# Row maxima and exponentials taken by pairs over two PSUM banks, a second bank for the rotated projections, the opening of expert pages on GpSimd, and side steps at other places of the turn

## The chip, the cores and the metric

The kernel runs on one core of one Trainium2 chip. The metric is the device time of one execution in microseconds, the median of several runs. The core has five engines with queues of their own: PE (TensorE, matmuls), DVE (VectorE), ACT (ScalarE), POOL (GpSimd) and SP (SyncE, which here only issues DMAs). They meet by semaphores.

## What is computed

One transformer block over 16 sequences of 512 positions, 128 channels wide: a layernorm modulated by a condition vector, causal attention of 16 heads with 8 channels each, a gated residual, a second modulated layernorm, and a mixture of 160 experts of which each position takes 8, with a shared expert beside them.

```python
h = _layernorm(x, axis=-1) * (1 + ca) + sa
x = x + ga * attn(h)        # rope on q and k, causal softmax(q k / sqrt(8)) v, projection
h = _layernorm(x, axis=-1) * (1 + cb) + sb
x = x + gb * ffn(h)         # sigmoid router, top 8 of 160, silu experts of width 64, a shared expert
```

## The kernel before

The program is written out in full for each engine: there are no loops at run time. It has two phases. The first is attention with routing, in turns (`turn_a`, i from -2 to 16), one sequence further in each. The second runs the experts over pages of 128 rows, from about 1200 us on; the change leaves it alone.

**One turn.** `core(i)` is the backbone: 20 steps, each with a pair of *max units* of sequence i+1 and a pair of *exp units* of sequences i-1 and i. A unit is one PSUM bank of 512 scores, in causal pieces of heads of one parity (even heads stand on 64 partitions, odd ones on the other 64, so the two units of a pair hold the two halves of PE). Each quarter of a sequence (a quad, 4 heads, `c`) has ten units (`UNITS`), five pairs. In a max unit PE makes the scores (L569) and hides the upper triangle by small matmuls (L577, L582); then DVE takes the row maximum of each block of 128 (`reduce`, L598). The maxima go back into the operands as further rows (`max_end`, L609 to L643), so that in an exp unit PE's products (L680, hidden by L692) come out with the maximum subtracted, and ACT takes the exponential into `prob` (`expo`, L707). `attend` then multiplies by v (L743, bank 5), and ACT and DVE normalise (L752, L764, L769), one quad later, in between the pairs.

**Banks.** Of the eight PSUM banks two belong to the max units (`MX`, unit g in bank g % 2), three to the exp units (`ST`, unit g in bank 2 + g % 3), one to `attend` (`PV`), and one each to the steps before attention (`MA`) and after it (`MB`). PE's `begin` holds a unit back until the unit that had its bank is done with:

```python
wait(e, s_mxd, n * 4 * UNITS + g - 1)           # max unit g: unit g-2 is reduced
wait(e, s_exa, n * 4 * UNITS + g - prev + 1)    # exp unit g: unit g-3 has its exponential
```

`pair(u0, u1)` orders PE's work as: wait and first product of u0, wait and first product of u1, then the remaining products and hiding matmuls in turn.

**Side steps.** All else of the turn is cut into steps that `merge` places between the backbone's by a number from 0 to 1: `pre(i+2)` (layernorm, the projections q, q rotated, k, k rotated and v, all through bank `MA`: L452, L463, L518, with DVE's rope L458, L467 between them; and the split into bf16 parts with POOL's L486, L495), the loads and stores of SP (`exp_loads` L661, `max_loads` L551, stores L507, `clears` L382), the routing of sequences i-1 and i-2 (`to_logits`, `post`), and POOL's scatters of rows into pages (L818), paced by the backbone's semaphores. `PRE_AT`, `FIRST_AT`, `SECOND_AT` and their `_LATE` are the tables of places. An engine takes its steps strictly in this order.

**Paging.** In `post`, eleven DVE operations on one partition of 160 values (`paging`, L1036 to L1051) turn the counts of rows for each expert into page places. The last four (`fill`, `curd1`, `curd2`, `open`) prepare what the next sequence starts from. `keep` then writes the row positions twice, as `pos_s` (L1142, for the scatters) and `pos_all` (L1143, for the expert phase).

## Time and profile before

| | |
|---|---|
| median of 3 runs | 2020.71 us (2019.48 to 2025.43) |
| the profiled execution | 2040.86 us, of which the span of the trace is 2038.9 us |
| PE, DVE, ACT, POOL busy in the span | 77%, 58%, 41%, 50% |
| mean granted TensorE clock | 0.887 |
| first and last L609 (end of a sequence's maxima) | 87.7 and 1099.5 us, 16 of them |

The first 1100 us or so are the turns and the rest, from about 1200 us, the experts. The interval from one L609 to the next is the length of a turn. Busy shares alone say little here, since each engine waits for the others within a step; the questions are what each pair of units waits for, and how long the things take that the change joins or moves.

### The profile page before, as it was taken

What the parts mean: (1) busy time and instruction counts of PE and PEld (TensorE: products, weight loads), DVE (VectorE), ACT (ScalarE), POOL (GpSimd) and SP (SyncE); (2) the same over time, 40 slices, a digit from 0 to 9 for tenths busy, and PEclk for the clock granted to TensorE, in tenths of its full rate; (3) what the DMA queues carried; (4) which work ended last, traced back from release to release, by engine and by line L of the source; (5) the groups of instructions that cost most, each with busy time, mean ns of one, the idle gap of its engine ahead of it and who ended that gap; (6) DMA issues with size and microseconds to landing.
All of it is one profiled execution on the core that took longest, in us unless ns stands there. A gap on an engine that the chain in (4) does not pass through costs nothing.

```text
span 2038.9 us, 35388 instructions
## 1 busy us (share of the span) xinstructions
PE 1565.4 (77%) x12102; PEld 792.8 (39%) x12102; DVE 1185.1 (58%) x2998; ACT 826.2 (41%) x1717; POOL 1021.8 (50%) x1057
## 2 busy tenths in 40 slices
PE   5558877788788778877877668966888888888875
PEld 2224433343343334333333345643444444444431
DVE  4657876687678767777766526633444444444434
ACT  1045544453445445445544434323343333343421
POOL 2001355555665556555645510056666666666663
PEclk9989888997898779778977678978999999999988
DMA  5695455554555545545542258986777777777631
GB/s 161 178 303 159 140 150 149 167 158 141 158 167 157 143 135 168 143 140 170 168 113 74 79 188 283 334 274 185 240 237 229 212 240 222 239 239 239 207 106 56
DMA packets 264986, 369.70 MB, mean 181 GB/s; under 512 B 41207, under 2 KB 141832, under 8 KB 264680
## 3 DMA queue, kind: packets, MB, share of 16 engines
q1 hardware_dynamic: 214248, 268.81, 45.5%
q0 software_dynamic: 28672, 58.78, 9.5%
q10 hardware_dynamic: 21888, 39.86, 5.2%
q8 instruction: 98, 1.61, 0.3%
q14 instruction: 80, 0.66, 0.1%
HBM read 219.69 MB, written 147.60 MB: 180 GB/s over the span
## 4 chain that ended last, share of the span: by engine, by line
PE 46%; DVE 20%; issue 12%; another core or an unknown queue 12%; ACT 5%; SPq 2%; DMA 2%; ACTq 1%; POOL 1%; DVEq 0%
DVE block_max L598 9%; PE bank L1715 6%; PE bank L743 5%; PE bank L1739 4%; PE bank L1578 4%; PE bank L1557 3%; PE bank L1594 3%; PE bank L569 3%; PE bank L680 2%; ACT prob L707 2%; PE bank L692 2%; PE bank L452 2%; PE bank L582 2%; PE bank L1720 1%
## 5 line engine op out<-in xcount | busy, mean ns | idle before, releaser
L1646 POOL DMA_INDIRECT vh<-results,pos_all x448 | 454.3, 1014 | 351.6 <-PE bank L1313 125.3
L818 POOL DMA_INDIRECT pages<-h,pos_s x448 | 433.2, 967 | 262.5 <-issue 103.7
L598 DVE TENSOR_REDUCE block_max<-bank 128x4 f32<-128x512 f32 x640 | 411.9, 683 | 245.7 <-PE bank L582 112.6
L707 ACT ACTIVATE prob<-bank 128x512 f32<-128x512 f32 x640 | 349.4, 598 | 465.9 <-PE bank L692 245.3
L1733 DVE TENSOR_TENSOR work<-work,bank 128x512 f32<-128x512 f32 x160 | 110.1, 688 | 358.1 <-issue 187.8
L569 PE MATMUL bank<-km,qm 64*128 64x512 bf16 (+3 forms) x1024 | 203.2, 343 | 112.2 <-DVE block_max L598 65.7
L680 PE MATMUL bank<-qe,ke 64*128 64x512 bf16 (+3 forms) x1024 | 174.9, 341 | 96.3 <-issue 57.2
L743 PE MATMUL bank<-prob,v_ext 128*32 128x512 f32 (+3 forms) x2048 | 225.7, 506 | 8.3 <-issue 5.3
L1608 ACT ACTIVATE v_ext<-bank 128x256 f32<-128x256 f32 x254 | 87.0, 387 | 199.9 <-remote 84.3
L569 PEld LDWEIGHTS bank<-km,qm 64*128 64x128 bf16 x1024 | 51.6, 97 | 276.6 <-issue 164.6
L1594 PE MATMUL bank<-prob,ke 64*128 64x128 f32 x1216 | 114.4, 309 | 52.3 <-ACT ke L1586 37.0
L1727 ACT ACTIVATE work<-bank 128x512 f32<-128x512 f32 x160 | 96.2, 601 | 143.2 <-PE bank L1715 77.2
L1594 PEld LDWEIGHTS bank<-prob,ke 64*128 64x128 f32 x1216 | 84.8, 197 | 141.5 <-issue 84.1
L680 PEld LDWEIGHTS bank<-qe,ke 64*128 64x128 bf16 x1024 | 50.1, 99 | 224.0 <-issue 153.9
L1715 PE MATMUL bank<-vh,on_att 128*128 128x512 f32 x160 | 88.4, 636 | 35.4 <-issue 28.5
L1578 PE MATMUL bank<-qe,prob 128*64 128x128 f32 x1216 | 105.3, 297 | 12.5 <-issue 9.2
L692 PE MATMUL bank<-cb_all 64*128 64x128 bf16 (+1 forms) x1280 | 112.6, 226 | 0.0
L1557 PE MATMUL bank<-c_all,prob 128*128 128x128 f32 x608 | 104.8, 297 | 2.9 <-issue 1.5
L1586 ACT ACTIVATE ke<-bank 128x256 f32<-128x256 f32 x152 | 58.6, 385 | 117.7 <-remote 71.0
L413 POOL TENSOR_TENSOR rstd<-var,mhalf 128x4 f32<-128x4 f32 x16 | 16.5, 1032 | 162.8 <-DVE var L407 162.8
L486 POOL TENSOR_TENSOR work<-work,shelf 128x512 f32<-128x512 f32 x32 | 36.9, 1153 | 121.6 <-ACT shelf L480 121.6
L692 PEld LDWEIGHTS bank<-cb_all 64*128 64x128 bf16 x1280 | 75.3, 106 | 31.1 <-issue 11.7
(221 smaller groups left out, 2542.4 us busy)
## 6 DMA issues: line engine op xcount, KB each, us to landing
prob<-wexp SPq DMA_DIRECT2D x448, 96.0 KB
pages<-free_rows SPq DMA_DIRECT2D x38, 1024.0 KB
prob<-pages SPq DMA_DIRECT2D x152, 256.0 KB
results<-v_ext ACTq DMA_DIRECT2D x152, 256.0 KB
qm<-q_stacks SPq DMA_DIRECT2D x64, 256.0 KB
km<-k_stacks SPq DMA_DIRECT2D x64, 256.0 KB
qe<-q_stacks SPq DMA_DIRECT2D x64, 256.0 KB
ke<-k_stacks SPq DMA_DIRECT2D x64, 256.0 KB
```

The lines of the kernel that those rows point to most:

```text
L569: e.matmul(MX[g % 2][:, c0:c0 + (i + 1) * P], qm[rows_, c % 2, h, i * P:(i + 1) * P], km[rows_, c % 2, h, 0:(i + 1) * P], start=(k == 0), ...
L598: e.tensor_reduce(block_max[:, at, :], MX[g % 2][:, :].rearrange("p (k t) -> p k t", t=P), AX.X, ALU.max).then_inc(s_mxd, 1)
L680: e.matmul(ST[g % 3][:, c0:c0 + S - j * P], ke[rows_, c % 2, h, j * P:(j + 1) * P], qe[rows_, c % 2, h, j * P:S], start=(k == 0), stop=Tru ...
L692: return e.matmul(out_, pick[rows_, :], over, start=False, stop=True, skip_group_check=True)
L707: e.activation(prob[:, slot, :], ST[g % 3][:, :], ACT.Exp, scale=SCALE).then_inc(s_exa, 1)
L743: last = e.matmul(PV[32 * g:32 * g + 32, j * P:S], v_ext[:, j, 4 * c + g, :], prob[:, (c % 2) * UNITS + u, c0:c0 + S - j * P], start=(j == ...
L818: e.indirect_dma_start(out=pages, in_=h2[:, t, :], in_offset=None, out_offset=bass.IndirectOffsetOnAxis(ap=pos_s[:, t * TOPK + k:t * TOPK ...
L1557: last = e.transpose(TX[G % 2][:, :].rearrange("d (p q) -> d q p", q=GRP)[:, q, :], x_in[G % DEEP][:, q, :], ident)
L1578: last = e.matmul(GT[half:half + 64, (j // 2) * P:(j // 2 + 1) * P], w_gate(G, j), x_T[G % 2][:, j * P:(j + 1) * P], start=True, stop=True)
L1594: last = e.matmul(YP[j % 2][:, (j // 2) * D:(j // 2 + 1) * D], h_g[G % 2][half:half + 64, (j // 2) * P:(j // 2 + 1) * P], w_down(G, j), st ...
L1646: e.indirect_dma_start(out=y8[:, i, k, :], out_offset=None, in_=results[0:ready(n) * GRP * P, :], in_offset=bass.IndirectOffsetOnAxis(ap=p ...
L1715: e.matmul(FG[:, :], fw[v % 4][:, c0:c0 + P], vh[:, PAGED + m, :], start=True, stop=True).then_inc(s_dg, 1)
```

## The change

1. The two max units of a pair, now always in `max_banks[:, 0]` and `[:, 1]`, raise one semaphore, and DVE reduces both with one instruction. PE starts a pair when the whole pair before it is reduced. Likewise the exp units: two banks instead of three, one exponential of 1024 columns for a pair, and PE starts a pair when the exponential of the whole pair before it is done. The semaphores count pairs.
2. The bank that this frees (`MC`, bank 4) takes the rotated projections. So the second projection of q no longer waits for DVE to have read the first, and k's first waits for q's first only.
3. `fill`, `curd1`, `curd2` and `open` leave DVE; six operations on POOL (`open_pages`) take their place.
4. `pos_s` is gone; the scatters read `pos_all`.
5. The tables of places are other ones, also for SP's loads; `SECOND_AT` has 13 entries, not 14, and the pacing of scatters ends at 0.306 of a turn, not 0.4.

```diff
-        block_max = sb("block_max", [P, 40, NT])
+        block_max = sb("block_max", [P, 2, 20, NT])
...
-        pos_s = sb("pos_s", [P, NT * TOPK], U32)
...
+        opened = sb("opened", [1, NE])
-        bank = [ctx.enter_context(nc.psum_tensor(f"bank{i}", [P, 512], F32)) for i in range(8)]
-        MX, ST, PV, MA, MB = bank[0:2], bank[2:5], bank[5], bank[6], bank[7]
+        max_banks = ctx.enter_context(nc.psum_tensor("max_banks", [P, 2, S], F32))
+        exp_banks = ctx.enter_context(nc.psum_tensor("exp_banks", [P, 2, S], F32))
+        bank = [b[:, i, :] for b in (max_banks, exp_banks) for i in range(2)] + \
+            [ctx.enter_context(nc.psum_tensor(f"bank{i}", [P, 512], F32)) for i in range(4, 8)]
+        MX, ST, MC, PV, MA, MB = bank[0:2], bank[2:4], bank[4], bank[5], bank[6], bank[7]
...
                 def proj_a(e, w=w, prev=prev):
...
-                        pre_d.wait(e, prev + "_b", n)
+                        pre_d.wait(e, prev + "_a", n)
                     pre_p.done(e.matmul(MA[:, :], col["w" + w], hT[:, :], start=True, stop=True), w + "_a")
...
                 def proj_b(e, w=w):
-                    pre_d.wait(e, w + "_a", n)
-                    pre_p.done(e.matmul(MA[:, :], col["w" + w + "r"], hT[:, :], start=True, stop=True), w + "_b")
+                    if w == "k":
+                        pre_d.wait(e, "q_b", n)
+                    else:
+                        pre_d.wait(e, "k_b", n - 1)
+                    pre_p.done(e.matmul(MC[:, :], col["w" + w + "r"], hT[:, :], start=True, stop=True), w + "_b")
...
             def v_proj(e):
-                pre_d.wait(e, "k_b", n)
+                pre_d.wait(e, "k_a", n)
...
         def max_unit(n, g):
...
-                wait(e, s_mxd, n * 4 * UNITS + g - 1)
+                wait(e, s_mxd, n * 2 * UNITS + g // 2)
...
-                    hide(e, 1).then_inc(s_mxp, 1)
+                    last = hide(e, 1)
+                    if u % 2 == 1:
+                        last.then_inc(s_mxp, 1)
             def reduce(e):
-                e.wait_ge(s_mxp, n * 4 * UNITS + g + 1)
-                if g == 0:
+                if u % 2 == 0:
+                    return
+                e.wait_ge(s_mxp, n * 2 * UNITS + g // 2 + 1)
+                if g == 1:
                     fin_d.wait(e, "i0", n - 1)
-                at = (u % 4 // 2 * 16 + par * 8 + 2 * c + u // 4) if u < 8 else 32 + 4 * par + c
-                e.tensor_reduce(block_max[:, at, :], MX[g % 2][:, :].rearrange("p (k t) -> p k t", t=P),
+                at = (u % 4 // 2 * 8 + 2 * c + u // 4) if u < 8 else 16 + c
+                e.tensor_reduce(block_max[:, :, at, :], max_banks[:, :, :].rearrange("p b (k t) -> p b k t", t=P),
                                 AX.X, ALU.max).then_inc(s_mxd, 1)
...
         def exp_unit(n, g):
...
-            prev = 3 if g >= 3 else g + 4 * UNITS - max(k for k in range(4 * UNITS) if k % 3 == g % 3)
...
-                wait(e, s_exa, n * 4 * UNITS + g - prev + 1)
+                wait(e, s_exa, n * 2 * UNITS + g // 2)
...
             def expo(e):
-                e.wait_ge(s_exp, n * 4 * UNITS + g + 1)
-                if u == 0:
+                if par == 0:
+                    return
+                e.wait_ge(s_exp, n * 2 * UNITS + g // 2 + 1)
+                if u == 1:
                     wait(e, s_pv, 4 * n + c - 1)
-                slot = (c % 2) * UNITS + exp_place(pieces[0][0], par, pieces[0][1])[0]
-                e.activation(prob[:, slot, :], ST[g % 3][:, :], ACT.Exp, scale=SCALE).then_inc(s_exa, 1)
+                slot = (c % 2) * UNITS + exp_place(pieces[0][0], 0, pieces[0][1])[0]
+                e.activation(prob[:, slot:slot + 2, :], exp_banks[:, :, :], ACT.Exp, scale=SCALE).then_inc(s_exa, 1)
...
-                ("filled", lambda e: e.tensor_scalar(filled[:, :], fill[:, :], -float(P), None, ALU.add)),
-                ("fill", lambda e: e.scalar_tensor_tensor(out=fill[:, :], in0=newp[:, :], scalar=-float(P),
-                                                          in1=total[:, :], op0=ALU.mult, op1=ALU.add)),
-                ("curd1", lambda e: e.scalar_tensor_tensor(out=curd[:, :], in0=endp[:, now, :], scalar=float(P),
-                                                           in1=rows[:, now, 1, :], op0=ALU.mult, op1=ALU.subtract)),
-                ("curd2", lambda e: e.scalar_tensor_tensor(out=curd[:, :], in0=newp[:, :], scalar=0.0, in1=curd[:, :],
-                                                           op0=ALU.is_gt, op1=ALU.mult)),
-                ("open", lambda e: e.tensor_tensor(rows[:, then, 1, :], rows[:, now, 1, :], curd[:, :], ALU.add)))
+                ("filled", lambda e: e.tensor_scalar(filled[:, :], fill[:, :], -float(P), None, ALU.add)))
+
+            any_row = eb_row[:, :]
+            opening = (
+                ("taken", lambda e: e.tensor_scalar(opened[:, :], newp[:, :], float(P), None, ALU.mult)),
+                ("any", lambda e: e.tensor_scalar(any_row, newp[:, :], 1.0, None, ALU.min)),
+                ("fill", lambda e: e.tensor_tensor(fill[:, :], total[:, :], opened[:, :], ALU.subtract)),
+                ("past", lambda e: e.tensor_tensor(opened[:, :], rows[:, now, 0, :], opened[:, :], ALU.add)),
+                ("last", lambda e: e.tensor_tensor(opened[:, :], opened[:, :], any_row, ALU.mult)),
+                ("open", lambda e: e.tensor_tensor(rows[:, then, 1, :], rows[:, now, 1, :], opened[:, :], ALU.add)))
...
                 if k == 0:
                     P_.wait(e, "cnt", n)
+                    G_.wait(e, "open", n - 1)
...
+            def open_pages(e):
+                D_.wait(e, "filled", n)
+                for k, (name, f) in enumerate(opening):
+                    if k > 1:
+                        G_.wait(e, opening[k - 1][0], n)
+                    G_.done(f(e), name)
...
-            steps.append({"pe": spread, "act": spread_keep, "sp": lambda e: ends_store(e, n)})
+            steps.append({"pe": spread, "act": spread_keep, "pool": open_pages, "sp": lambda e: ends_store(e, n)})
...
             def keep(e):
                 D_.wait(e, "pos1", n)
-                wait(e, s_scat, 16 * NT * TOPK * n)
-                D_.done(e.tensor_scalar(pos_s[:, :], pos8[:, :, :].rearrange("p t k -> p (t k)"), -TAKEN, None, ALU.add), "pos_s")
...
-        PRE_AT = (0.021, 0.061, 0.15, 0.207, 0.274, 0.36, 0.422, 0.474, 0.481, 0.553, 0.611, 0.636, 0.688, 0.751)
+        PRE_AT = (0.030, 0.085, 0.163, 0.227, 0.303, 0.351, 0.425, 0.475, 0.477, 0.558, 0.616, 0.654, 0.692, 0.752)
...
-                streams.append((exp_loads(i, (0,)), 0.03, 0.03))
-                streams.append((exp_loads(i, (1,)), 0.28, 0.28))
-                streams.append((exp_loads(i, (2,)), 0.53, 0.53))
-                streams.append((exp_loads(i, (3,)), 0.78, 0.78))
+                streams.append((exp_loads(i, (0,)), 0.101, 0.101))
+                streams.append((exp_loads(i, (1,)), 0.223, 0.223))
+                streams.append((exp_loads(i, (2,)), 0.546, 0.546))
+                streams.append((exp_loads(i, (3,)), 0.640, 0.640))
```

The table `PRE_AT` stands for the others (`PRE_LATE`, `FIRST_AT`, `FIRST_LATE`, `SECOND_AT`, `SECOND_LATE`), most of whose entries move by less than 0.03 of a turn.

On **PE**, in the middle of a steady turn, between the products with v of one quad (L743; L754 in the new numbering), stand a max pair and an exp pair. `bank0` and `bank1` are `MX`, `bank2` to `bank4` are `ST`. Before:

```order
L743 MATMUL bank5<-prob,v_ext 32x128 [waits s_exa]
L743 MATMUL bank5<-prob,v_ext 32x128 x3
L569 MATMUL bank0<-km,qm 128x512 [waits s_mxd]
L569 MATMUL bank1<-km,qm 128x512 [waits s_mxd]
L577 MATMUL bank0<-cb_all 128x64
...
L743 MATMUL bank5<-prob,v_ext 32x256 x3
L680 MATMUL bank2<-qe,ke 128x512 [waits s_exa]
L680 MATMUL bank3<-qe,ke 128x512 [waits s_exa]
L692 MATMUL bank2<-cb_all 128x64
```

and now, at the same place:

```order
L754 MATMUL bank5<-prob,v_ext 32x128 [waits s_exa]
L754 MATMUL bank5<-prob,v_ext 32x128 x3
L574 MATMUL max_banks<-km,qm 128x512 [waits s_mxd] x2
L582 MATMUL max_banks<-cb_all 128x64 x4
L754 MATMUL bank5<-prob,v_ext 32x256 [waits s_exa]
L754 MATMUL bank5<-prob,v_ext 32x256 x3
L687 MATMUL exp_banks<-qe,ke 128x512 [waits s_exa] x2
L699 MATMUL exp_banks<-cb_all 128x64 x4
```

PE's matmuls and their order are the same; what the waits of L574 and L687 ask for is now a whole pair, and the exp pair uses the same two banks each time.

On **DVE**, at the paging of a steady turn (names: `fill`, `total`, `newp` and `endp` are rows of 160 counts). Before:

```order
L1039 SCALAR_TENSOR_TENSOR endp<-newp,endp,zero_row 1x160 [waits post_d,s_ends]
L1041 TENSOR_TENSOR curd<-endp,newp 1x160 [waits post_d]
L1042 SCALAR_TENSOR_TENSOR rows_deep<-curd,rows_deep 1x160 [waits post_d]
L598 TENSOR_REDUCE block_max<-bank 128x4 [waits s_mxp] x2
L421 TENSOR_SCALAR work<-xr,mv,rstd 128x128 x2
L1044 TENSOR_SCALAR filled_deep<-fill 1x160 [waits post_p]
L1045 SCALAR_TENSOR_TENSOR fill<-newp,total 1x160 [waits post_d]
L1047 SCALAR_TENSOR_TENSOR curd<-endp,rows_deep 1x160 [waits post_d]
L1049 SCALAR_TENSOR_TENSOR curd<-newp,curd 1x160 [waits post_d]
L1051 TENSOR_TENSOR rows_deep<-rows_deep,curd 1x160 [waits post_d]
L598 TENSOR_REDUCE block_max<-bank 128x4 [waits s_mxp] x2
```

and now on DVE:

```order
L1050 SCALAR_TENSOR_TENSOR endp<-newp,endp,zero_row 1x160 [waits s_ends,post_d]
L1052 TENSOR_TENSOR curd<-endp,newp 1x160 [waits post_d]
L1053 SCALAR_TENSOR_TENSOR rows_deep<-curd,rows_deep 1x160 [waits post_d]
L607 TENSOR_REDUCE block_max<-max_banks 128x2x4 [waits s_mxp]
L1055 TENSOR_SCALAR filled_deep<-fill 1x160 [waits post_p]
L423 TENSOR_SCALAR work<-xr,mv,rstd 128x128 x2
L607 TENSOR_REDUCE block_max<-max_banks 128x2x4 [waits s_mxp]
```

with these on POOL, between two scatters (L829) of sequence i-2's rows:

```order
L1059 TENSOR_SCALAR opened<-newp 1x160 [waits post_d]
L1060 TENSOR_SCALAR eb_row<-newp 1x160
L1061 TENSOR_TENSOR fill<-total,opened 1x160 [waits post_g]
L1062 TENSOR_TENSOR opened<-rows_deep,opened 1x160 [waits post_g]
L1063 TENSOR_TENSOR opened<-opened,eb_row 1x160 [waits post_g]
L1064 TENSOR_TENSOR rows_deep<-rows_deep,opened 1x160 [waits post_g]
L829 DMA pages<-h,pos_all 77824x128 [waits s_mxp]
```

Four operations went from ahead of a reduction on DVE, and six came in ahead of a scatter on POOL.

## Rows read from the trace of the kernel before

**Rows 1.** The page: busy time of each engine in the span
```profile
PE 1565.4 (77%) x12102; PEld 792.8 (39%) x12102; DVE 1185.1 (58%) x2998; ACT 826.2 (41%) x1717; POOL 1021.8 (50%) x1057
```
**Rows 2.** Windows, one turn: length; PE, PEld, DVE, ACT, POOL busy; clock
```profile
476.10:545.60 69.50, 55.24 (x506) 26.59 (x505) 50.62 (x148) 31.76 (x63) 39.60 (x43) 0.84 0.53 154
```
**Rows 3.** The chain that ended last, 290 to 965 us, shares by line
```profile
by line: DVE block_max L598 17.2%; issue 11.4%; PE bank L743 8.5%; another core or an unknown queue 5.0%; PE bank L569 4.8%; PE bank L680 4.7%; PE bank L692 3.2%; PE bank L452 3.1%; PE bank L582 2.9%; ACT prob L707 2.4%; PE bank L950 1.9%; 
```
**Rows 4.** Waits, 290 to 965 us: who for whom, us, times, longest
```profile
PEld bank L569 <- DVE block_max L598: 36.5, 81, 1.5
...
PEld bank L680 <- ACT prob L707: 30.9, 35, 6.4
...
PE bank L569 <- DVE block_max L598: 28.0, 56, 1.5
...
PE bank L680 <- ACT prob L707: 14.3, 4, 6.2
```
**Rows 5.** Groups of instructions by shape: busy us, mean ns
```profile
L598 DVE TENSOR_REDUCE block_max<-bank 128x4 f32<-128x512 f32 x640 | 411.9, 683 | 245.7 <-PE bank L582 112.6 <-remote 89.8 <-PE bank L577 39.9
L707 ACT ACTIVATE prob<-bank 128x512 f32<-128x512 f32 x640 | 349.4, 598 | 465.9 <-PE bank L692 245.3 <-remote 211.6 <-issue 7.0
...
L1656 DVE TENSOR_TENSOR vh<-vh,wts_all 128x1024 f32<-128x1024 f32 x56 | 68.4, 1221 | 0.1
...
L1568 ACT ACTIVATE qe<-bank 128x512 f32<-128x512 f32 x102 | 61.3, 601 | 40.1 <-remote 29.9 <-PE bank L1557 9.2 <-issue 1.0
L1586 ACT ACTIVATE ke<-bank 128x256 f32<-128x256 f32 x152 | 58.6, 385 | 117.7 <-remote 71.0 <-PE bank L1578 38.6 <-issue 8.0
...
L1664 DVE TENSOR_TENSOR vh<-vh 128x512 f32<-128x512 f32 x56 | 38.5, 687 | 0.3
```
**Rows 6.** Timeline, one step of a turn: start us, us
```profile
502.46 1.28 DVE L598 TENSOR_REDUCE block_max<-bank 128x4 f32<-128x512 f32 x2
502.99 1.08 ACT L707 ACTIVATE prob<-bank 128x512 f32<-128x512 f32 x2 [2.11 <-PE bank L692]
...
503.20 0.39 PE L569 MATMUL bank<-km,qm 64*128 64x512 bf16 x1 [0.43 <-DVE block_max L598]
...
503.80 0.39 PE L569 MATMUL bank<-km,qm 64*128 64x512 bf16 x1 [0.21 <-DVE block_max L598]
```
**Rows 7.** Timeline, DVE's four last paging operations
```profile
627.75 0.31 DVE L1045 SCALAR_TENSOR_TENSOR fill<-newp,total 1x160 f32<-1x160 f32 x1
...
628.80 0.31 DVE L1051 TENSOR_TENSOR rows_deep<-rows_deep,curd 1x160 f32<-1x160 f32 x1
```
**Rows 8.** Timeline: pos_s and pos_all on DVE, the smallest operations on POOL
```profile
509.24 0.17 DVE L1142 TENSOR_SCALAR pos_s<-pos 128x32 uint32<-128x32 f32 x1
509.32 0.18 DVE L1143 TENSOR_SCALAR pos_all<-pos 128x32 uint32<-128x32 f32 x1
...
510.82 0.45 POOL L1158 TENSOR_TENSOR hit<-hit 128x128 f32<-128x128 f32 x1
...
511.73 0.25 POOL L1162 TENSOR_TENSOR wts_all<-hit 128x32 f32<-128x32 f32 x1
```
**Rows 9.** The line L463 (rotated projections): what PE waited for, whole span
```profile
  DVE work L458: 10.3, 8
```
**Rows 10.** Timeline, the stall near a turn's end
```profile
601.95 0.39 PE L680 MATMUL bank<-qe,ke 64*128 64x512 bf16 x1 [0.87 <-issue]
...
604.84 1.09 ACT L707 ACTIVATE prob<-bank 128x512 f32<-128x512 f32 x2 [6.06 <-remote]
605.01 1.29 DVE L598 TENSOR_REDUCE block_max<-bank 128x4 f32<-128x512 f32 x2 [5.19 <-remote]
...
605.49 0.61 PE L680 MATMUL bank<-qe,ke 64*128 64x512 bf16 x1 [3.16 <-issue]
```
**Rows 11.** Windows ahead of and behind that stall
```profile
605.50:621.50 16.00, 12.64 (x84) 5.35 (x84) 13.14 (x55) 6.06 (x13) 6.59 (x8) 0.50 0.38 97
587.60:601.60 14.00, 11.96 (x131) 6.67 (x131) 9.55 (x29) 8.94 (x18) 11.21 (x12) 1.00 0.56 182
```

More of the change, by code:

```diff
@@ L814, in scatter @@
             if t == 0 and k == 0:
-                post_d.wait(e, "pos_s", n)
+                post_d.wait(e, "pos_all", n)
                 post_a.wait(e, "h2", n)
@@ L1062, in page_op @@
                     wait(e, s_ends, 16 * n)
-                    D_.wait(e, "curd1", n - 1)
                 if name == "filled":
```

83 lines of the change are left out of this document (40 added, 43 removed).

## The prediction, made before the changed kernel was timed

> **What bounds the kernel now.** I read the page first: no engine is full, PE is busy for 77% of the span and DVE for 58% [rows 1]. That is a mean over two phases, and the change touches the turns alone. So next the windows of one turn: of 69.5 us PE is busy for 55.2, DVE for 50.6, ACT for 31.8, POOL for 39.6, at a granted clock of 0.84 [rows 2]. PE and DVE are both near what the turn takes, ACT and POOL are not. The chain over some ten turns says which of them the end hangs on: 17.2% of it is DVE's reductions, the largest share of any line, while the exponentials have 2.4%; 11.4% is "issue", time in which PE waits for nothing that is shown [rows 3]. The waits agree: PE's loads for the max units waited 81 times for DVE and its matmuls 56 times, for the exp units 35 and 4 times for ACT [rows 4]. The timeline of one step shows how this goes: DVE takes two reductions in 1.28 us from 502.46, PE's first product starts at 503.20, behind the first of them, its second only at 503.80, behind the other [rows 6]. A step is thus a loop from PE to DVE and back, with side work of both between.
>
> **Joining the reductions.** A pair costs 1.28 us [rows 6]. One of 1024 columns isn't in the trace. DVE's other operation of that length takes 1221 ns against 687 for 512 columns, so 534 ns for 512 more; with 683 for the reduction of one bank that is 1217 ns [rows 5]. 320 pairs by 0.06 us are 20 us of DVE's time. The bound on the one side is nothing (no gain from joining), on the other the whole fixed part of an operation, 687 - 534 = 153 ns a pair, 49 us. PE loses nothing of its own by waiting for the whole pair: its first product now starts later, but the second, which ended last anyway, starts up to 0.06 us earlier.
>
> **Joining the exponentials.** Two cost 1.08 us [rows 6]; one of 1024 columns, by ACT's 601 ns for 512 and 385 for 256, is 598 + 2 * 216 = 1030 ns [rows 5]: 0.05 us by 320, 16 us of ACT. With ACT's exponentials at 2.4% of the chain, about 16 of 675 us, where they are busy for some 390 * 0.598 = 233 (40 a turn, and 675 / 69 = 9.8 turns), a fifteenth of that counts: 1 us. The Trainium skill ("ScalarE: Activation LUTs", section "What ACT_TABLE_LOAD costs") gives 186 ns fixed, 0.833 ns a column and an overlap of 93 ns between neighbours. By that the saving would be 93 ns a pair, 30 us of ACT and 2 us of the sum; our rows of 1.08 us show less to be saved, and I stay with them.
>
> **Paging and pos_s.** DVE's four last paging operations run from 627.75 to 629.11, 1.36 us [rows 7], in 14 sequences: 19 us. `pos_s` delays what follows by 0.08 us [rows 8], 1 us in all. So DVE is relieved of 20 + 19 + 1 = 40 us. What share of it counts? In the 675 us of the chain's window L598 has 116 us [rows 3]; its instructions there are about 40 in 69 us by 683 ns, 267 us busy. So 43% of DVE's time lies on the chain, and of 40 us I take 17.
>
> **POOL.** Six operations on one partition of 160 values, each behind a wait for the one before. The nearest rows are 0.25 us for 32 columns and 0.45 for 128, on 128 partitions [rows 8]: 1.5 to 3 us a turn. They stand ahead of a scatter, and behind the wait for `filled`. POOL idles for 30 us of a turn [rows 2], which hides them, and their results are needed a turn later: 0. If that cover were gone (a scatter that ACT's `back_keep` awaits becomes late), it is at most 14 * 3 = 42 us.
>
> **The bank MC.** The rotated projections no longer wait for DVE's rope of the plain ones. PE waited 10.3 us for that in the whole span [rows 9]. The bounds are 0 and 10.3; I take half, 5 us, since DVE's own work stays.
>
> **The third exp bank.** This is the price. Before, the second product of a pair waited for the first exponential of the pair before, now for both: 1030 - 598 = 0.43 us later, wherever PE was held by ACT. Rows name 39 such waits in 675 us [rows 4]; over the sixteen sequences' turns that makes some 64, by 0.43 us 27 us. Behind an exp pair PE meets a max pair, and there it often waits for DVE (81 to 137 waits on some 195 pairs [rows 4]), which absorbs the delay. I take 60% as absorbed: +11 us. The bounds are 0 and all 320 pairs, 137 us.
>
> **The places.** PE's order of matmuls is nearly the same, the side steps move by a row or a few. SP's load of the fourth quad now stands at 0.640 and waits there for its buffer, free at about 0.735; behind it on SP stand a clear and k's store, which have until the next turn. I cost that at 0: the first loads needed have a quarter turn. What the moves are worth elsewhere has no row. Their nearest measure is the stall that recurs near a turn's end, 3.16 us on PE [rows 10]: gone in fifteen turns it would be 47 us, doubled as much the other way. I take 0 and keep both.
>
> **The sum.** -17 - 1 - 5 + 11 = -12 us on the profiled execution's 2040.86, so 2029. That execution stands 20 us above the median of the runs shown, 2020.7; the same 12 us off the median give **2008**.
>
> **The rivals.**
>
> *The exp pair becomes the loop (slower).* With one set of banks, PE's exp pair, ACT's exponential and PE's next exp pair can't overlap at all. Every lateness of ACT (its side steps, 0.6 us and more each, stand in one queue with the exponentials) is passed on to PE undamped. For it: the four waits of PE for ACT took 14.3 us, up to 6.2 each [rows 4], and some of the "issue" ahead of L680 may be ACT's. Against it: ACT is busy for under half the turn. My gains are 23 us, so it decides once 54 pairs of 320 pass on 0.43 us. If a third do, 107 pairs, it is 46 - 23 = +23 us: 2044.
>
> *DVE's relief becomes idleness (no change).* If the step's length is PE's own work and its unexplained waits, what DVE saves is waited away, and -5 meets +11 with a remnant of the 17: 2015 to 2027, say 2021. The chain's 11.4% of "issue" speaks for it, the 17.2% of reductions against.
>
> *The stall and the clock (much faster).* In the stall DVE and ACT both sit idle for over 5 us until about 605, and PE resumes at 605.49 [rows 10]. Before it the clock was 1.00 (2.4 GHz), in the 16 us behind it 0.50 (1.2 GHz) [rows 11], and the same 512-column product takes 0.61 us instead of 0.39 [rows 10]. At a mean of 0.84, a third of the turn runs at half clock [rows 2]. In 16 us there PE is busy for 12.6; at full clock this would be 12.6 * 0.39 / 0.61 = 8.1, 4.5 us less [rows 11]. If other places break the stall in most turns, and half of that reaches the end, it is 2.3 + 0.5 * 3.16, some 3.9 us in ten turns: 2008 - 39, about 1970. Against it: nothing in the change names the stall's cause. The Trainium skill ("TensorE: Matmul & The Clock Gate", section "HAM oscillation — how this bites in real kernels") says that pauses of PE put it to half rate, paid again at each. By this rule the trace agrees here, with half clock right behind the stall; the same rule makes it dearer if single exp banks add pauses.
>
> *The change doesn't do what it says:* the PSUM operand over two banks could be taken more slowly than its columns. At 1.28 us for the joined reduction and 1.08 for the exponential nothing is won there, and the sum is -12 + 9 + 1 = -2, in with "no change".
>
> **The numbers.** Within 0.3%, 6 us, is what a measurement of this kernel can't tell from no change. Chances: forecast 0.41, stall and clock 0.12, no change 0.17 (with the change that doesn't do what it says), the exp pair 0.30. Faster is thus 0.53, the same 0.17, slower 0.30. The range reaches to about 1965, the stall's rival, and to 2045, the exp rival at a third of the pairs; beyond stand more pairs than that, or a POOL without cover, 2 in 10 or less. The likeliest case's own range is 1990 to 2014: DVE's full 40 us on the chain and none of it.
>
> **What would show it.** Right: the joined reduction near 1.22 us and the exponential near 1.03, DVE's busy time 35 to 45 us lower, the line of reductions still the largest on the chain, L468's wait for DVE gone, waits of the exp products for ACT up to 60 or 80 per ten turns and no more than 0.5 us each on the whole. Wrong: turns (from one end of maxima to the next) that are longer than 69 us with PE waiting for ACT in most exp pairs; or a row of scatters or `rstd` late on POOL behind the opening; or a mean clock in the turns away from 0.85 by more than 0.03, which would say that pauses of PE, and not the joined operations, made the difference.

## The result, and the profile after

| | before | changed |
|---|---|---|
| median | 2022.12 us (2019.48 to 2025.43, 4 runs) | 2061.60 us (2060.28 to 2063.01, 4 runs) |
| ratio | | 1.0195 (95%: 1.0172 to 1.0219), slower; whether by 2% is within the noise |
| span of the profiled execution | 2038.9 us | 2061.2 us |

The profiled execution of before stands 19 us above its median, that of the changed kernel 1 us above. So the two traces differ by 22 us only; the other 17 us of the 39.5 between the medians can't be placed in them.

The page of the changed kernel, against [rows 1]:

```profile
PE 1513.2 (73%) x12102; PEld 774.4 (38%) x12102; DVE 1156.2 (56%) x2608; ACT 809.0 (39%) x1397; POOL 1076.8 (52%) x1141
```

DVE has 29 us less to do, ACT 17, and POOL 55 more. The joined operations cost what rows of before had said (1217 and 1030 ns), namely 1220 and 1024 ns (by shape; busy us, mean ns | idle before, and what ended it), against [rows 5]:

```profile
L607 DVE TENSOR_REDUCE block_max<-max_banks 128x8 f32<-128x1024 f32 x320 | 390.5, 1220 | 295.7 <-remote 153.8 <-PE max_banks L587 99.9 <-PE max_banks L582 33.2
L718 ACT ACTIVATE prob<-exp_banks 128x1024 f32<-128x1024 f32 x320 | 327.6, 1024 | 459.3 <-PE exp_banks L699 268.3 <-remote 178.7 <-issue 9.7
```

So less work, and yet more time. The windows say where: one steady turn, against [rows 2].

```profile
479.30:552.10 72.80, 50.05 (x505) 24.91 (x505) 49.08 (x124) 31.93 (x46) 44.54 (x50) 0.85 0.56 149
```

72.8 us for 69.5, at the same clock (0.85, 0.84). Counted by the ends of the maxima (L617, before L609), the changed kernel is ahead by 3 us at the first, 4.6 at the second and 5.1 at the third (199.87 against 204.99), in turns that have no scatters yet; it then loses some 3 us in most turns and stands 28 us behind at the last (1127.70 against 1099.55). The experts behind it take no longer (933.5 against 939.4 us).

The waits of PE, 290 to 965 us, against [rows 4] (us in total, times, longest):

```profile
PE max_banks L574 <- DVE block_max L607: 79.8, 76, 2.7
PE exp_banks L687 <- issue: 45.8, 25, 5.1
PE exp_banks L687 <- ACT prob L718: 34.6, 23, 7.2
PE bank L1035 <- DVE chosen L999: 14.7, 8, 1.8
```

PE's matmuls wait for DVE three times as long as before (28.0), for ACT more than twice (14.3), and newly for the choice of experts (L999) ahead of the count. But DVE is not busier. What DVE waits for says more. DVE's waits, 337 to 1055 us, first of before, then of the changed kernel:

```profile
DVE block_max L598 <- PE bank L582: 63.7, 36, 3.8
DVE block_max L598 <- remote: 63.3, 23, 5.4
```

```profile
DVE block_max L607 <- remote: 125.6, 37, 8.0
DVE block_max L607 <- PE max_banks L587: 50.5, 31, 4.7
```

"Remote" is an idle time at whose end no instruction of this core ended: by the profile, the operand had been there for long. It doubled. The same word stood in [rows 5] already, 89.8 us ahead of the reductions and 211.6 ahead of the exponentials, and I had read past it. What it is, the timeline of the changed kernel shows near a turn's end (the place of [rows 10]):

```profile
607.72 0.28 PE L699 MATMUL exp_banks<-cb_all 64*128 64x128 bf16 x4
...
608.51 0.22 PE L582 MATMUL max_banks<-cb_all 64*128 64x64 bf16 x4
...
612.61 0.96 POOL L829 DMA_INDIRECT pages<-h,pos_all  x1 [0.30 <-issue]
613.72 1.02 ACT L718 ACTIVATE prob<-exp_banks 128x1024 f32<-128x1024 f32 x1 [6.06 <-remote]
...
614.80 0.61 PE L687 MATMUL exp_banks<-qe,ke 64*128 64x512 bf16 x2 [5.06 <-issue]
...
616.62 1.23 DVE L607 TENSOR_REDUCE block_max<-max_banks 128x8 f32<-128x1024 f32 x1 [7.92 <-remote]
```

The exp pair is ready at 608.00; its exponential starts at 613.72. The max pair is ready at 608.73; its reduction starts at 616.62. ACT and DVE are idle all the while, and so, from 609.7, is PE. I call this a **late signal**.

The trace holds more than its views show: the time of each semaphore's update. In the kernel before, 912 of the 2385 updates that PE gave came over 0.3 us behind the last end of a matmul that gives that semaphore, none of them ahead of the first scatter. Of the 2941 updates by ACT, DVE and POOL not one did. So it is what comes from PE that is late, and the reader starts at once when it comes. Whether PE's signal is late or the matmul's result itself can't be told, since the profile models the ends of matmuls; "ready" above is by such an end.

The Trainium skill ("Perfetto Trace Analysis", section "Per-instruction lifecycle: what the profiler-reported window actually captures") says that waiting for a semaphore and its propagation lie outside what a profiled instruction shows. By that, such a delay has no row of its own, and the trace agrees: in the views it shows only as idle time with no cause on the core (6.06 and 7.92 us above).

### The profile page after: what moved, and what is told of

Same layout as the page of the kernel before. It is cut to its first block and busy times, and to the rows that moved or that the text cites. A ratio compares the mean times of both kernels' runs of the same rounds, so it can differ in the third digit from the quotient of the medians.

```text
span 2061.2 us, 34762 instructions
## 1 busy us (share of the span) xinstructions
PE 1513.2 (73%) x12102; PEld 774.4 (38%) x12102; DVE 1156.2 (56%) x2608; ACT 809.0 (39%) x1397; POOL 1076.8 (52%) x1141
## 3 DMA queue, kind: packets, MB, share of 16 engines
q0 software_dynamic: 28672, 58.78, 9.4%
## 5 line engine op out<-in xcount | busy, mean ns | idle before, releaser
L829 POOL DMA_INDIRECT pages<-h,pos_all x448 | 438.7, 979 | 225.4 <-issue 123.7
L607 DVE TENSOR_REDUCE block_max<-max_banks 128x8 f32<-128x1024 f32 x320 | 390.5, 1220 | 295.7 <-remote 153.8
L718 ACT ACTIVATE prob<-exp_banks 128x1024 f32<-128x1024 f32 x320 | 327.6, 1024 | 459.3 <-PE exp_banks L699 268.3
L574 PE MATMUL max_banks<-km,qm 64*128 64x512 bf16 (+3 forms) x1024 | 145.9, 347 | 182.2 <-DVE block_max L607 149.7
L754 PE MATMUL bank<-prob,v_ext 128*32 128x512 f32 (+3 forms) x2048 | 229.7, 502 | 11.9 <-issue 9.5
L687 PE MATMUL exp_banks<-qe,ke 64*128 64x512 bf16 (+3 forms) x1024 | 144.1, 342 | 126.2 <-issue 61.0
L1609 PE MATMUL exp_banks<-prob,ke 64*128 64x128 f32 x608 | 115.9, 315 | 46.7 <-ACT ke L1601 23.9
L574 PEld LDWEIGHTS max_banks<-km,qm 64*128 64x128 bf16 x1024 | 37.5, 98 | 297.4 <-DVE block_max L607 154.4
L687 PEld LDWEIGHTS exp_banks<-qe,ke 64*128 64x128 bf16 x1024 | 39.5, 100 | 240.9 <-issue 164.7
L1593 PE MATMUL exp_banks<-qe,prob 128*64 128x128 f32 x1216 | 105.0, 296 | 10.6 <-issue 7.3
L1572 PE MATMUL max_banks<-c_all,prob 128*128 128x128 f32 x608 | 104.8, 297 | 1.2 <-issue 0.9
L699 PE MATMUL exp_banks<-cb_all 64*128 64x128 bf16 (+1 forms) x1280 | 91.8, 225 | 0.0
L1754 PE MATMUL bank<-work,on_att 128*128 128x512 f32 x160 | 89.9, 645 | 0.0
```

The lines of the kernel that those rows point to most:

```text
L574: e.matmul(MX[par][:, c0:c0 + (i + 1) * P], qm[rows_, c % 2, h, i * P:(i + 1) * P], km[rows_, c % 2, h, 0:(i + 1) * P], start=(k == 0), st ...
L607: e.tensor_reduce(block_max[:, :, at, :], max_banks[:, :, :].rearrange("p b (k t) -> p b k t", t=P), AX.X, ALU.max).then_inc(s_mxd, 1)
L687: e.matmul(ST[par][:, c0:c0 + S - j * P], ke[rows_, c % 2, h, j * P:(j + 1) * P], qe[rows_, c % 2, h, j * P:S], start=(k == 0), stop=True, ...
L718: e.activation(prob[:, slot:slot + 2, :], exp_banks[:, :, :], ACT.Exp, scale=SCALE).then_inc(s_exa, 1)
L754: last = e.matmul(PV[32 * g:32 * g + 32, j * P:S], v_ext[:, j, 4 * c + g, :], prob[:, (c % 2) * UNITS + u, c0:c0 + S - j * P], start=(j == ...
L829: e.indirect_dma_start(out=pages, in_=h2[:, t, :], in_offset=None, out_offset=bass.IndirectOffsetOnAxis(ap=pos_all[:, n, t * TOPK + k:t * ...
```

## The experiments

They ran in five batches, each on another chip, and the kernel before ran beside them each time. Its median tells the chips apart: 2024 to 2043 us on four, as in the main comparison (2022), and 1784 us on one. No batch was repeated on its chip, so a lasting property of a chip can't be told from its condition at that time. Ratios are to before on the same chip. "Remote" is the sum of the profile's rows on the reductions and on the exponentials (DVE + ACT, us); "none" is said of these two groups.

| run | what it is | ratio (95%) | before there | remote |
|---|---|---|---|---|
| changed kernel | | 1.0195 (1.0172 to 1.0219) | 2022 | 153.8 + 178.7 |
| a_old_places | changed, all old places | 1.0106 (1.0074 to 1.0139) | 2040 | 86.5 + 177.7 |
| c_new_places | before, all new places | 1.0259 (1.0227 to 1.0291) | 2040 | 139.5 + 212.9 |
| d_open_pool | before, opening on POOL | 1.0046 (1.0022 to 1.0069) | 2040 | 91.5 + 210.9 |
| e_max_pairs | before, maxima by pairs | 0.9971 (0.9953 to 0.9989) | 2040 | 81.5 + 201.6 |
| after_again | changed | **0.9920** (0.9898 to 0.9943) | **1784** | none |
| g_pairs_only | changed, old places, opening on DVE | 1.0016 (0.9994 to 1.0037) | 1784 | none |
| f_exp_pairs | before, exponentials by pairs | 1.0116 (1.0081 to 1.0150) | 1784 | none |
| n_choose_back | changed, cut and choice back | 0.9909 (0.9890 to 0.9929) | 1784 | none |
| t_first_back | changed, first half's places back | 1.0080 (1.0051 to 1.0109) | 2042 | 118.3 + 195.9 |
| t_pre_back | changed, `PRE_*` back | 1.0304 (1.0272 to 1.0335) | 2042 | 134.4 + 236.9 |
| t_loads_back | changed, SP's loads back | 1.0215 (1.0179 to 1.0251) | 2042 | 145.4 + 177.7 |
| t_second_back | changed, `SECOND_*` back | 1.0178 (1.0150 to 1.0207) | 2042 | 147.7 + 220.0 |
| x_before_plain | before, plain DMAs for the scatters | 0.9350 (0.9326 to 0.9375) | 2024 | none |
| x_after_plain | changed, plain DMAs for the scatters | 0.9269 (0.9245 to 0.9293) | 2024 | none |
| p_first_new | before, first half's new places | 0.9969 (0.9950 to 0.9988) | 2024 | 98.7 + 174.6 |
| u_two_back | changed, first half's places and opening back | 1.0097 (1.0069 to 1.0125) | 2024 | 102.3 + 147.0 |
| y_max_first | before, maxima by pairs and first half's new places | 0.9967 (0.9945 to 0.9988) | 2043 | 99.4 + 166.7 |
| f_exp_again | before, exponentials by pairs | 1.0072 (1.0050 to 1.0093) | 2043 | 68.8 + 130.7 |

**Parts and places.** Three theories: the single set of exp banks, POOL's opening, or the places. The expectations name times by the main comparison's 2022 us; ratios go over to another chip better.

> The changed kernel with the places of before: the same tables of side steps, loads and pacing (one of the two entries 0.175 for paging dropped, since there are three paging steps now). Theory 'single exp set' (the third exp bank's loss costs the 3 us a turn): stays at 2050 to 2065. Theory 'opening on POOL' (the six operations, 3.5 us a turn on POOL, delay scatters or the row they stand ahead of): also 2050 to 2065. Theory 'places' (the new tables cost it): falls by 25 to 45, to 2020 or 2035, and PE's new waits at the count for `chosen` (some 2 us a turn) are gone. Those waits alone, 14 by 2, would be 28 us.

The edit, and the reverse of it in c_new_places:

```diff
-        FIRST_AT = (0.519, 0.548, 0.562, 0.646, 0.675, 0.678, 0.703, 0.734, 0.766, 0.792, 0.824, 0.850, 0.858, 0.902, 0.902, 0.978, 0.982)
+        FIRST_AT = (0.535, 0.548, 0.573, 0.646, 0.668, 0.721, 0.723, 0.729, 0.776, 0.796, 0.85, 0.851, 0.859, 0.909,
+                    0.91, 0.939, 0.964)
...
```

> The kernel before with the new places alone (the fourth paging step right beside the third). Theory 'places': slower by 20 to 40, 2042 to 2062, PE waits for `chosen` ahead of the count. Theories 'single exp set' and 'opening on POOL': within 8 of before, 2014 to 2030.

> The kernel before with the opening on POOL alone. Theory 'opening on POOL': slower by 20 to 45, 2042 to 2067, all in turns with scatters. Theories 'single exp set' and 'places': DVE's 19 us of relief by its 43% share of the chain, so faster by 0 to 10, 2012 to 2022; POOL's busy time 50 us higher, without effect.

```diff
-            steps.append({"pe": spread, "act": spread_keep, "sp": lambda e: ends_store(e, n)})
+            steps.append({"pe": spread, "act": spread_keep, "pool": open_pages, "sp": lambda e: ends_store(e, n)})
```

> The kernel before with the maxima by pairs alone (and the scatters reading pos_all): three single exp banks, opening on DVE, old places. All three theories: the joined reduction costs 1.22 us for 1.28, so 20 us of DVE by 43%: faster by 5 to 12, 2010 to 2017. If instead the loss lies in the joined maxima (PE's first product of a pair now waits for the whole pair), it is slower, 2030 to 2060, with long waits of L574's successor for DVE.

```diff
-                e.tensor_reduce(block_max[:, at, :], MX[g % 2][:, :].rearrange("p (k t) -> p k t", t=P),
+                e.tensor_reduce(block_max[:, :, at, :], max_banks[:, :, :].rearrange("p b (k t) -> p b k t", t=P),
```

The places are a large part: 0.009 of the changed kernel's 1.0195 (give or take 0.004, and from two chips), and 1.0259 when put on the kernel before. With them goes the remote idle time of DVE, 86.5 us with old places against 153.8 in the changed kernel, and 139.5 with new places against 89.8 in the kernel before. With the old places:

```profile
L607 DVE TENSOR_REDUCE block_max<-max_banks 128x8 f32<-128x1024 f32 x320 | 390.6, 1221 | 280.5 <-PE max_banks L587 121.0 <-remote 86.5 <-PE max_banks L582 54.5
```

and with the new ones on the kernel before:

```profile
L598 DVE TENSOR_REDUCE block_max<-bank 128x4 f32<-128x512 f32 x640 | 412.0, 683 | 272.1 <-remote 139.5 <-PE bank L582 96.8 <-PE bank L577 29.4
```

No theory was borne out in size. With the old places the changed kernel came down by 18 us, where the theory of the places asked for 25 to 45 and the others for none. The kernel before went up by 53 with the new ones, more than the 20 to 40 expected. The opening cost 9, under the 20 to 45 of its own theory. Only the joined maxima came in as expected (0.9971, so 6 us faster).

The opening costs 1.0046, where all theories but its own had 0.995 to 1.0: DVE's busy time fell by 16 us (to 1168.9; 19 was asked), and nothing was paid for it. Its six operations run one after another from 566.78 to 570.68 us, 3.9 us, on POOL, which issues the scatters:

```profile
566.78 0.63 POOL L1059 TENSOR_SCALAR opened<-newp 1x160 f32<-1x160 f32 x1
567.40 0.61 POOL L1060 TENSOR_SCALAR eb_row<-newp 1x160 f32<-1x160 f32 x1
568.09 0.51 POOL L1061 TENSOR_TENSOR fill<-total,opened 1x160 f32<-1x160 f32 x1
...
569.87 0.81 POOL L1064 TENSOR_TENSOR rows_deep<-rows_deep,opened 1x160 f32<-1x160 f32 x1
```

The two left out are of the kind of L1061, 0.51 and 0.52 us. I had taken 0.25 to 0.5 us for one. The Trainium skill ("GPSIMD Engine Reference", section "3.1 Elementwise — side-by-side cycle accounting") gives 2.6 cycles an element at 1.2 GHz for two inputs; for 160 elements that is an estimate of 0.35 us before any fixed part. The trace agrees in so far as the two-input operations, 0.51 us at the least, lie above it; what the rest is no run here shows, and the one-input ones took no less (0.61 and 0.63).

**The same kernel on another chip.** The next runs were meant to size what was left.

> The changed kernel again, as the measure for the others on this chip. 1.0195 of before as first measured; between 1.014 and 1.025.

> The changed kernel with the opening on DVE and the places of before: what is left is both joinings, the bank MC and pos_s. With the old places and the opening on POOL the ratio was 1.0106, and the opening alone cost 1.0046. Theory 'single exp set': 1.004 to 1.010, turns of 70 to 71 us, PE waiting some 6 us a turn for ACT. Theory 'the opening is all that is left': 0.995 to 1.002.

> The kernel before with the exponentials by pairs alone (and the scatters reading pos_all), bank 4 unused, single maxima. Theory 'single exp set': slower by 10 to 35, 1.005 to 1.017, with more waits of PE's exp products for ACT. My prediction's terms give -1 + 11 = +10, its rival +23 and more. Theory 'joined units are both harmless alone': 0.997 to 1.003.

```diff
-                e.activation(prob[:, slot, :], ST[g % 3][:, :], ACT.Exp, scale=SCALE).then_inc(s_exa, 1)
+                e.activation(prob[:, slot:slot + 2, :], exp_banks[:, :, :], ACT.Exp, scale=SCALE).then_inc(s_exa, 1)
```

> The changed kernel with its last two routing steps of a turn (the second cut and the choice) back from 0.978 and 0.982 to 0.939 and 0.964, nothing else. Theory 'the late choice is what the new places cost': PE's waits for it at the count (some 2 us a turn, 14 turns) go, ratio lower than the changed kernel's by 0.007 to 0.013. Rival, 'it only stands ahead of another wait' (PE would meet DVE or ACT a few rows on): within 0.003 of the changed kernel.

The first of these expectations was missed altogether, and that opened the case: here the kernel before takes 1784 us and the changed kernel 1771, **13 us less**. The prediction's sum was -12. The same two groups, on this chip:

```profile
L607 DVE TENSOR_REDUCE block_max<-max_banks 128x8 f32<-128x1024 f32 x320 | 390.0, 1219 | 141.2 <-PE max_banks L587 85.4 <-PE max_banks L582 50.3 <-issue 0.5
L718 ACT ACTIVATE prob<-exp_banks 128x1024 f32<-128x1024 f32 x320 | 327.4, 1023 | 262.3 <-PE exp_banks L699 251.2 <-issue 6.2
```

The joined operations take the same time to 1 ns; "remote" is gone, and of 1968 updates that PE gave none was over 0.3 us late. The timeline at the same place of the program as above:

```profile
538.97 0.28 PE L699 MATMUL exp_banks<-cb_all 64*128 64x128 bf16 x4
...
539.29 1.02 ACT L718 ACTIVATE prob<-exp_banks 128x1024 f32<-128x1024 f32 x1 [0.79 <-issue]
...
539.76 0.22 PE L582 MATMUL max_banks<-cb_all 64*128 64x64 bf16 x4
...
540.03 1.23 DVE L607 TENSOR_REDUCE block_max<-max_banks 128x8 f32<-128x1024 f32 x1 [0.48 <-PE max_banks L582]
```

0.04 us from the end of the exp pair to the exponential, where it was 5.72. The turn takes 58.3 us instead of 71.8:

```profile
487.83:546.10 58.27, 46.89 (x505) 23.27 (x505) 48.93 (x124) 31.41 (x46) 44.39 (x50) 0.91 0.66 187
```

With g at 1.0016, the new places and the opening together gain 0.010 here, where they lost. The joined exponentials alone cost 1.0116, as their theory said: a real price, but one that the other parts pay for here. The choice moved back (n) changes nothing here, as its rival said.

**Which table.** Back on a chip with late signals (before 2042 us):

> The changed kernel with the places of the first routing half back. Two chips have shown two pictures: where before takes 2020 to 2040 us (long stops of PE at fixed places of the turn), all new places together cost the changed kernel 0.009 of before; where before takes 1784 us (no such stops) the changed kernel is at 0.992. Theory 'one table carries it, the first half's' (late choice, 2 us a turn of waits): on a chip with stops 1.008 to 1.014 instead of 1.0195. Theory 'the stops carry it, and any table shifts them': 1.013 to 1.022. On a chip without stops both say 0.989 to 0.996.

> The changed kernel with the places of the steps before attention back. Theory 'first half': stays at 1.017 to 1.022 on a chip with stops. Theory 'the stops': the stop of a turn stands after the 17th pair of maxima, where these steps end in the stores of k; 10.1 us from the 17th to the 18th reduction in the changed kernel, 7.3 with all old places. If this table moves it, 1.010 to 1.016 and under 8.5 us there. Without stops 0.989 to 0.998.

> The changed kernel with the five places of SP's loads back. Theory 'first half': 1.017 to 1.022 on a chip with stops. Theory 'the loads': an earlier fourth load blocks SP, so that the store of k is issued later and its burst meets PE's fetch; 1.010 to 1.016. Without stops 0.989 to 0.996.

> The changed kernel with the places of the second routing half back (and its pacing left). Both theories of the first half and of the loads: unchanged, 1.017 to 1.022 on a chip with stops, 0.989 to 0.996 without. If this table carries it, 1.008 to 1.014 with stops.

The first routing half's places carry it: 1.0080, as low as with all old places. Those of `SECOND_*` and of the loads don't, and the new `PRE_*` even help by 0.011. That was in no theory. The pacing of the scatters and the place of the maxima's end were not moved back by themselves. I had blamed the late choice; but with it back, PE still waited for `chosen` for 10.6 us in ten turns, and what fell was DVE's remote time, 153.8 to 118.3. Where in the turn it lies I worked out from the timelines, as the time from one reduction's end to the next, median of eight turns: from the 17th pair to the 18th it is 7.4 us before, 10.1 in the changed kernel, about 7 with all old places and with those of the first half (single turns 3 to 9), and 2.8 on the chip without late signals.

The sum of "remote" is no price list, though. The kernel before with joined exponentials, run again below (f_exp_again), has 199.5 us of it and is slower than before (1.0072), the kernel before with the first half's new places has 273.3 and is faster (0.9969).

**What the signals are late for.** In the program none is late until the first scatter: in before the first scatter is at 237.2 us and the first exponential over 0.3 us late at 241.5, in the changed kernel 231.8 and 236.0. The next two kernels leave out the rows' way to their experts' pages: the same 64 KB go to fixed places, by a plain DMA in place of the indirect one.

> The kernel before with its 448 scatters (rows to computed places, through POOL's indirect DMA) replaced by plain DMAs of the same 64 KB to fixed places of the same pages, issued by POOL at the same points of the order; the rows thus don't go to the pages of their experts. Theory 'late signals come with the scatters': DVE and ACT start up to 8 us after PE's last matmul, in 212 us of before's turns, only after the first scatter of the program; with plain DMAs this falls under 30 us and the turns from 68.5 to under 60 us. Rival 'late signals come with the traffic of DRAM as such': 150 us or more stay. On a chip without late signals: 0.99 to 1.01 of before by POOL's lighter work.

> The changed kernel with the same replacement. Theory 'late signals turn the verdict': over the kernel before with plain DMAs its time is 0.987 to 0.996, as on the chip without late signals (0.992), wherever it runs. Rival 'the places cost by themselves on such chips': 1.01 or more over the kernel before with plain DMAs.

```diff
-            e.indirect_dma_start(
-                out=pages, in_=h2[:, t, :], in_offset=None,
-                out_offset=bass.IndirectOffsetOnAxis(ap=pos_all[:, n, t * TOPK + k:t * TOPK + k + 1], axis=0),
-            ).then_inc(s_scat, 16)
+            first = (n * NT * TOPK + t * TOPK + k) * P
+            e.dma_start(pages[first:first + P, :], h2[:, t, :]).then_inc(s_scat, 16)
```

On a chip with late signals (before 2024 us) they vanish from the turns of both kernels. The groups of before with plain DMAs, and then of the changed kernel with them:

```profile
L598 DVE TENSOR_REDUCE block_max<-bank 128x4 f32<-128x512 f32 x640 | 410.5, 682 | 146.2 <-PE bank L582 108.2 <-PE bank L577 37.8
L707 ACT ACTIVATE prob<-bank 128x512 f32<-128x512 f32 x640 | 347.9, 599 | 274.8 <-PE bank L692 274.2
L819 POOL DMA_DIRECT2D pages<-h x448 | 243.1, 545 | 282.0 <-PE bank L692 119.0 <-PE bank L582 102.0 <-PE bank L577 42.6
```

```profile
L607 DVE TENSOR_REDUCE block_max<-max_banks 128x8 f32<-128x1024 f32 x320 | 390.1, 1219 | 148.0 <-PE max_banks L587 99.2 <-PE max_banks L582 44.5
L718 ACT ACTIVATE prob<-exp_banks 128x1024 f32<-128x1024 f32 x320 | 327.7, 1024 | 286.0 <-PE exp_banks L699 281.1
L830 POOL DMA_DIRECT2D pages<-h x448 | 244.1, 548 | 185.9 <-PE exp_banks L699 72.2 <-PE max_banks L582 52.5 <-PE max_banks L587 40.6
```

The queue, its bytes (58.78 MB, half of them the scatters') and its packets (28672) are the same, so it is not the amount of traffic. Two things went together with the indirect form and aren't told apart: POOL is held for 548 instead of 979 ns by an issue, and the rows go to places side by side instead of scattered ones.

The same executions hold a second test that I hadn't planned. In the expert phase these kernels still gather rows by POOL's indirect DMAs, and there the late signals are back. In the kernel before with plain scatters, not one of 1565 updates by PE from 237 us on was over 0.3 us late until the first gather at 1188.1 us; from there on 373 of 566 were, the first at 1193.8. Two of ACT's groups in that phase:

```profile
L1606 ACT ACTIVATE v_ext<-bank 128x256 f32<-128x256 f32 x254 | 86.8, 384 | 214.7 <-PE bank L1592 90.5 <-remote 72.6 <-issue 51.2
...
L1584 ACT ACTIVATE ke<-bank 128x256 f32<-128x256 f32 x152 | 58.5, 385 | 120.1 <-remote 82.4 <-PE bank L1576 36.8 <-issue 0.9
```

From the first gather to the end it takes 702 us here and 707 in the kernel before as it was, so nearly all of what was won was won ahead of it.

The turns fall to about 60 and 59 us. And the verdict turns: 1879.01 / 1894.85 = **0.992** (about 0.988 to 0.995 by the two intervals), the value of the other chip. Both were foretold by the theory of late signals; the rivals named in the two expectations are out.

**Parts, again.**

> The kernel before with the new places of the first routing half alone. Putting them back in the changed kernel took 1.0195 to 1.008. Theory 'the first half's places cost it where signals are late': 1.008 to 1.02 on such a chip, 0.995 to 1.003 where none are late. Rival 'they cost only together with the single exp banks': 0.997 to 1.004 on either.

> The changed kernel with two parts back: the places of the first routing half, and the opening on DVE. A candidate for both kinds of chip. By 1.008 less 0.0046 for the opening: 1.001 to 1.006 where signals are late; 0.988 to 0.998 where none are.

> The exponentials by pairs alone, again, on this chip: 1.0116 where no signal was late. Theory 'late signals make the single set dear': 1.015 to 1.03 where they are late. Rival 'the set costs the same everywhere': 1.008 to 1.015. By differences of the runs on chips with late signals (1.0106 less 0.0046 for the opening, plus 0.003 for the maxima) it would be 1.009.

> The kernel before with the two parts that were each 0.997 of it where signals are late: maxima by pairs (0.9971) and the new places of the first routing half (0.9969). If the two add up: 0.992 to 0.996. If both take away the same wait (DVE ahead of the reductions at the turn's end): 0.996 to 0.999. Without late signals 0.985 to 0.998.

The rival held in the first: these places gain 0.003 on the kernel before and cost only in company. u_two_back was missed. With the first half's places back, the opening's return to DVE won nothing that shows (1.0097 against 1.0080), so the 1.0046 is no fixed price that could be subtracted. The joined exponentials alone cost 1.0072, not more than the 1.0116 without late signals; that theory falls. Whether the two single gains add up stays open: 0.9967 (0.9945 to 0.9988) was measured, 0.994 would be their sum, with as wide an interval. Where signals are late, this kernel is ahead of before and of the changed one, though of before by little more than such a comparison resolves; where none are late it was not run, and the changed kernel beats before by 0.008.

## Why the prediction was wrong

It forecast 2008 us, faster; the time is 2061.6, above the range's 2045. What it said about the length of the joined instructions held. Its sum, -12, was met on the chip that delivers signals at once (-13), but in part by luck: there the joined exponentials cost +21 instead of +10, and the places, costed at nothing, gained with the opening some 17. By its own steps, in us, on chips with late signals (ratio times 2040, each give or take 4 to 8; from two chips besides that of the main comparison):

| step | forecast | measured |
|---|---|---|
| joined reductions, pos_s | -9 | -6 (e alone, 0.9971) |
| opening: DVE's relief -8, POOL 0 | -8 | +9 (d alone, 1.0046) |
| joined exponentials with one set of banks | -1 + 11 | +15 (f alone, 1.0072) |
| bank MC and what the parts do together | -5 | +4 (what is left of a, 1.0106, by subtraction) |
| places | 0 | +18 (1.0195 less 1.0106) |
| sum | -12 | +39.5 |

- **The places: the first step that failed.** I took "0 and keep both", with the stall as the measure, at 3.16 us on PE and in sum 47 us a kernel; they cost 18. The stall was the right object, and its size was wrong: before has 301 us of remote idle time on the two groups of instructions alone, at several places of a turn, and with the moved side steps DVE's share of it went from 86.5 to 153.8 us. In the range I let the exp rival at 2045 stand for the slower side, and the stall's own bound of +47 (2055) didn't enter it. Even that would have been too low, since two more steps had the wrong sign.
- **The single exp set: right in sign, price half as large again.** +15 for +10. By itself it is some 15 of the 39.5 us, and it is as dear where no signal is late, so it doesn't turn the verdict. Its rival had +23 and the whole result for itself, by PE's waits for ACT in most exp pairs; they are 23 of PE's matmuls in 675 us, with up to 7.2 us each, against the 60 to 80 of no more than 0.5 us that I had called a sign of being right.
- **The opening: the second step that failed, by 17 us, cover that wasn't there.** POOL idles for 30 us of a turn [rows 2], but where the opening stands scatters come one upon the other, mostly with 0.3 us between. 3.9 us in one piece among them were priced at 1.5 to 3 and as hidden. Why they reach the end isn't shown; only that they do in d, and that taking them back won nothing in u_two_back.
- **DVE's relief.** It was 29 us, short of the 35 to 45 that I had named as a sign of being right. The rule of 43% fits the reductions (-6 of -9, give or take 4) and not the paging operations; that these stand where DVE waits in any case would explain it, and isn't shown.
- **The bank MC** was in no run by itself. PE's wait for DVE ahead of the rotated projections fell from 10.3 us [rows 9] to 2.5, but its unexplained idle time there ("issue") rose from 6.4 to 11.5, so little can have come of it.
- **The joined durations** (1220 and 1024 ns) **and the clock** of the turns (0.85 in the one shown) were right. Over the whole span the mean granted clock is lower (0.857 against 0.887), above all in the first 85 us (0.66 against 1.00), where the changed kernel is nevertheless ahead.
- **A slip in the range.** "1990 to 2014" for the likeliest case doesn't follow from its terms: DVE's 40 us wholly on the chain and not at all give 1985 and 2025.
- **The rival "the stall and the clock"** had the right cause with the wrong sign. I gave it 0.12 and only looked at what a stall gone would win.

What stays open: why the signals of PE come late on the other chips and not on one; whether it is the scattered places, POOL's longer issue or the indirect form itself; what beside the indirect scatters must coincide (the scatters run through most of a turn, but of PE's updates between 237 and 1100 us in the kernel before only a third, 415 of 1222, are over 0.3 us late); why the first half's places raise them only together with the joined banks.

## What to carry to other kernels

Idle time that ends "remote" ahead of a frequent instruction is a term of its own: add it up over its groups before costing an edit, since moved steps can change it by more than the operations saved, and take it as a range and not as a price. The same places of side steps gained on one chip and lost on others, so compare on several chips before believing 1% either way. Joining two operations saves little (0.06 us of 1.28 and of 1.08) and also joins their waits: with one set of banks for two that cost 0.7 to 1.2%, with late signals and without. "Idle elsewhere in the turn" hides nothing: look at the place where the moved operation will stand.

## What the runs showed that I had not expected

- The kernel before takes 1784 us on one chip and 2022 to 2043 on the others. In the changed kernel (1771 and 2062), traced on both kinds, reductions, exponentials and scatters take the same to 1 ns. The late signals are on one side only, also behind the turns (from its last maxima on: 827 us there, 933 here); that all of the difference follows from them isn't shown.
- Only what PE signals was late: 912 of 2385 updates in the kernel before, none of 2941 by ACT, DVE and POOL.
- POOL's indirect DMAs and late signals go together on such chips: idle times of up to 8.0 us behind a matmul's end in the turns, from 4.3 us after the first scatter; none with plain DMAs of the same bytes on the same queue, which are also issued in 548 instead of 979 ns; and again in the same execution from 5.7 us after the first indirect gather.
- One-partition operations of 160 values on POOL take 0.51 to 0.63 us by their medians, and up to 0.90 singly; on DVE they take 0.31 [rows 7].
